# A query projection moved ahead of a wait, and key stacks sent in three lots, in a fused attention kernel

## The reference

```python
# block 0: grouped-query attention, 32 query heads, 8 key/value heads, head width 16
q = x @ Wq + bq;  k = ctx @ Wk + bk;  v = ctx @ Wv + bv
scores = einsum('bkgld,bksd->bkgls', q, k) / sqrt(16) + mask
x = layernorm(softmax(scores) @ v @ Wo + bo + x) * gamma + beta
# block 1: two cross-attentions (16 heads of width 128, one extra key and value) and a gelu MLP
x = x + cross_attention(layernorm(x), ctx)      # twice
x = x + gelu(layernorm(x) @ w_fc1 + b_fc1) @ w_fc2 + b_fc2
```

## Time and profile before

| | |
|---|---|
| median of 3 runs | 2584.45 us (2582.57 to 2584.73) |
| profiled execution | 2582.68 us |
| TensorE busy | 2501.6 us, 97% |
| VectorE busy | 1700.4 us, 66% |
| ScalarE busy | 1496.3 us, 58% |
| GpSimd busy | 1325.7 us, 51% |
| block 0's pairs, batch 0 | from about 31 to 262 us |
| block 0's pairs, batch 1 | from about 1313 to 1547 us |

### The profile page before, as it was taken

How to read it: one execution, slowest core, us unless ns; L and a number is a source line. 1 busy time by engine, 2 the same in 40 slices (tenths; PEclk the granted TensorE clock), 3 DMA queues, 4 the chain that set the end, 5 groups by cost and what they waited for, 6 DMA issues and landing times.

```text
span 2580.9 us, 53158 instructions
## 1 busy us (share of the span) xinstructions
PE 2501.6 (97%) x19500; PEld 2067.1 (80%) x19500; DVE 1700.4 (66%) x2568; ACT 1496.3 (58%) x2360; POOL 1325.7 (51%) x778
## 2 busy tenths in 40 slices
PE   7999999999999999999989999999999999999999
PEld 6666788888888888888866667888888888888877
DVE  6999676666566666665269996656665665666541
ACT  5999455555555555555459994555545555555543
POOL 1255346665644666564603553566556456655644
PEclk8999999999999999999989999999999999999999
DMA  7222134544514455452462220345444144544522
GB/s 215 72 76 78 34 100 102 130 126 103 127 46 100 100 128 130 100 128 69 144 159 68 77 70 33 100 118 130 110 119 121 36 100 113 129 116 114 128 68 66
DMA packets 86916, 263.61 MB, mean 102 GB/s; under 512 B 20544, under 2 KB 26320, under 8 KB 81120
## 3 DMA queue, kind: packets, MB, share of 16 engines
q1 hardware_dynamic: 85760, 260.80, 38.2%
q10 hardware_dynamic: 992, 0.52, 0.1%
HBM read 135.39 MB, written 8.40 MB: 56 GB/s over the span
## 4 chain that ended last, share of the span: by engine, by line
PE 80%; DVE 10%; issue 4%; ACT 2%; POOL 1%; SPq 1%; DMA 1%; DVEq 0%; POOLq 0%; ACTq 0%
PE ps_m L1110 22%; PE ps_t L1110 19%; PE ps_s L1110 16%; PE ps_m L1379 7%; PE ps_t L1379 6%; DVE sm L1719 6%; PE ps_s L1232 3%; DVE pt L1727 1%; POOL pT_lo L561 1%; PE ps_m L1312 1%; PE ps_m L1268 1%; PE ps_m L1120 1%; PE ps_t L1251 1%; SPq L474 1%; DVE nm L1719 1%
## 5 line engine op out<-in xcount | busy, mean ns | idle before, releaser
L561 POOL TENSOR_TENSOR pT_lo<-pT_lo,pT_hi 128x1024 fp32r<-128x1024 f32 x220 | 530.0, 2409 | 498.0 <-ACT pT_hi L757 486.8
L757 ACT ACTIVATE pT_hi<-pT_lo 128x1024 fp32r<-128x1024 f32 x224 | 238.0, 1062 | 326.3 <-DMA pT_lo<-pb 326.3
L901 ACT ACTIVATE p<-ps_s,nm 128x1024 f32<-128x1024 f32 x256 | 284.9, 1113 | 206.5 <-DVE nm L1789 206.1
L1786 DVE TENSOR_REDUCE nmx<-ps_s 128x1 f32<-128x1024 f32 x256 | 309.8, 1210 | 121.9 <-PE ps_s L1110 121.9
L1110 PE MATMUL ps_s<-kT,qT 128*128 128x512 f32 x1536 | 384.0, 392 | 0.3 <-ACT p L901 0.3
L1805 DVE STREAM_TRANSPOSE pb<-p 128x1024 f32<-128x1024 f32 x224 | 278.1, 1242 | 107.0 <-ACT p L901 103.1
L1110 PEld LDWEIGHTS ps_s<-kT,qT 128*128 128x128 f32 x1536 | 281.3, 188 | 55.9 <-ACT p L901 1.3
L1719 DVE CUSTOM_DVE_ANT_0 sm<-ps_s,mask 128x1024 f32<-128x1024 f32 x256 | 302.7, 1214 | 14.1 <-PE ps_s L1232 12.7
L849 ACT ACTIVATE p<-sm,nm 128x1024 f32<-128x1024 f32 x256 | 293.5, 1146 | 22.5 <-DVE nm L1719 18.1
L1110 PE MATMUL ps_t<-ctxT,wa 128*128 128x512 f32 x1080 | 256.0, 390 | 0.0
L1110 PE MATMUL ps_m<-hT,wa 128*128 128x512 f32 x1008 | 243.9, 393 | 1.1 <-ACT g L1072 0.7
(11 more groups left out here) (181 smaller groups left out, 4667.3 us busy)
## 6 DMA issues: line engine op xcount, KB each, us to landing
pT_lo<-pb SPq DMA_DIRECT2D x896, 128.0 KB, 2.3
stg_qk<-in_wqk SPq DMA_DIRECT2D x40, 1024.0 KB, 7.4
stg_vo<-in_wo SPq DMA_DIRECT2D x48, 512.0 KB, 3.6
wob<-in_wo SPq DMA_DIRECT2D x32, 512.0 KB, 3.6
stg_vo<-in_wv SPq DMA_DIRECT2D x32, 512.0 KB, 3.7
q_stack<-scr_q SPq DMA_DIRECT2D x36, 128.0 KB, 4.2
st_ctx<-in_ctxT SPq DMA_DIRECT2D x8, 512.0 KB, 6.1
mask<-in_mask SPq DMA_DIRECT2D x8, 512.0 KB, 6.2
```

Of the source, the lines that this page charges most:

```text
L561: return nc.gpsimd.tensor_tensor(out, x, f32(hi), ALU.subtract)
L757: return nc.scalar.activation(out, in_, ACT.Copy)
L901: nc.scalar.activation(p[t % 2][:], ps_s[t % 2][:], ACT.Exp, bias=nm[:, i:i + 1], scale=SCALE1, accum_out=sums[:, i:i + 1]).then_inc(exp_d ...
L1786: nc.vector.tensor_reduce(nmx[:, i:i + 1], ps_s[t % 2][:], AX.X, ALU.max, negate=True)\
```

## The change

- Query column 3 is projected right behind column 2, before TensorE waits for the first stack, and no longer between `scores0(0)` and `scores0(1)`. ScalarE's `wide(b, 5)` now stands before `exp0(0)`, and VectorE's `low_part(5)` right behind the maxima of pair 0.
- Query columns 2 and 3 swap their banks: column 2 goes to `ps_m[1]`, column 3 to `ps_m[0]`. So the second turn waits for `low_part(4)`, and the first value products, which write `ps_m[0]`, for `low_part(5)`. Both columns wait for both key tiles to be freed.
- The key slices 1, 2 and 3 are sent one at a time, each behind the query stack and mask tile of the same number: 12 transfers of a third of the size, three times.

```diff
         bank0 = [ps_m[0][:], ps_m[1][:], ps_s[0][:, 0:512], ps_s[1][:, 0:512],
-                 ps_m[0][:], ps_m[1][:]]
+                 ps_m[1][:], ps_m[0][:]]
...
-                    if i == 1:
+                    if i >= 1:
                         for k in range(2):
                             sp.wait_ge(scr_k_out[k], 16 * (b + 1))
                             apart()
-                            stack_k(sp, k, slice(1, KVP), stack_rest)
+                            stack_k(sp, k, slice(i, i + 1), stack_rest)
...
-                for i in range(3, 5):
+                for i in range(3, 6):
                     wide(b, i)
...
                 exp0(0)
-                wide(b, 5)
                 exp0(1)
...
                     if i >= 2:
-                        free(nb + i)
+                        free(nb + 3)
...
-                pe.wait_ge(w0q_lo, CT * b + 3)
-                project_q0(2)
+                for i in range(2, 4):
+                    pe.wait_ge(w0q_lo, CT * b + i + 1)
+                    project_q0(i)
...
                         elif bank_of_half[2 * t + q] == 2:
-                            pe.wait_ge(bank_free, nb + U_PROJ0 + 2)
+                            pe.wait_ge(bank_free, nb + P_Q[2] + 3)
...
-                    if e == 0 and i == 0 and u >= 1:
-                        pe.wait_ge(rb0_done, u0 + u)
+                    if e == 0 and i == 0:
+                        if u >= 1:
+                            pe.wait_ge(rb0_done, u0 + u)
+                        else:
+                            pe.wait_ge(bank_free, nb + P_Q[3] + 3)
...
                 scores0(0)
-                pe.wait_ge(w0q_lo, CT * (b + 1))
-                project_q0(3)
                 scores0(1)
...
-                        pe.wait_ge(stack_rest, 16 * 30 * (b + 1))
+                        pe.wait_ge(stack_rest, 16 * 54 * (b + 1))
...
                 for t in range(2):
                     maxima0(t)
+                low_part(5)
...
-                    if t == 1:
-                        low_part(5)
                     copied0(t - 1, 1)
```

## The result

The changed kernel took 2569.12 us (median of 5 runs, 2569.01 to 2575.00) beside 2582.57 (5 runs, 2582.09 to 2584.73) for the kernel before on the same chip: ratio 0.9949, 95% interval 0.9938 to 0.9959. That is 13.45 us or 0.5% faster; forecast were 13.6 us. Measured a second time, the same kernel gave 0.9945 (0.9932 to 0.9958). The span of the profiled execution fell from 2580.9 to 2567.3 us.

A forecast was written before the change was run, and what follows sets the result against it. VectorE was taken to set the pace, leaving only start-up losses to win: 16.6 us, less 1.0 for the instruction block and 2.0 for the clock, gives 13.6, so 2570.8 us; range 2567 to 2577.5.

The forecast's parts named there:

- The bound: First attention: VectorE sets 3.51 us a pair of score tiles; only the 6.68 and 9.47 us lost earlier can be won.
- rival D: Steady stage takes the gain back because a transfer paced otherwise ends last: 2584.4 us, chance 0.05.
- Column 3 for nothing: TensorE's 3.02 us of column 3 fit the 3.43 us stack wait; moved ScalarE and VectorE parts free; first step 3.3 us.
- The turns' wait: TensorE's 3.02 us idle before the turns of tile 1 goes, since the swapped bank needs only low_part(4).
- The block: TensorE's stop before pair 5, read as late instructions behind key transfers, shrinks to 0.5 us a batch.
- upper bound: Instruction transfer still near the end of the shorter key burst, 47.6; TensorE goes on at 50.6: a stop of 2.0 us.
- clock term: One spell of TensorE's lower clock per batch stays, 1.0 us each, 2.0 in all; bounds 0 and 4.0.
- lower bound: No stop before pair 5: the instructions are asked for earlier, with only one or two key lots ahead.
- SyncE's queue: Issuing key lots 2 and 3 adds 5.5 us each; lot 3 still lands in time for pair 16: free.
- Rival E: Lot 3 lands late and scores of pair 16 wait; slower by 0.2% if landing after 97; 2590 us, chance 0.03.
- B: Stops before pair 5 stay, not caused by key stacks; lots give nothing: 10.4 us gained, 2574 us, chance 0.27.
- C: Lots 2 and 3 delay later blocks: one new stop a batch up to 2.67 us; 6.3 gained, 2578 us, chance 0.10.

The follow-up runs named there:

- e7: Changed kernel with the banks of columns 2 and 3 not swapped, low_part(5) still early: 2570.47 us.
- e5: Changed kernel plus 20 identity transposes on TensorE between scores0(0) and scores0(1), filling its wait for pair 0's maxima: 2569.64 us.
- e1: Changed kernel with key slices sent in one burst behind query stack 1, as before, so only the projection moved: 2577.96 us, again 2583.82 us.
- e4: Changed kernel with all three key slices in one burst of 12 transfers behind query stack 2: 2570.01 us.
- e6: Changed kernel with wide(b, 5) and low_part(5) back in their old places, banks still swapped: 2570.69 us.
- e8: Changed kernel with the bank swap undone and wide(b, 5) and low_part(5) back in their old places: 2572.05 us.
- e2: Kernel before with only the key slices sent in three lots, projection not moved: 2574.14 us, again 2574.19 us.

## Why the prediction was right, point by point

**The bound.** VectorE's pace of 3.51 us and the loss before it: 16.1 us before (6.68 + 9.47), 2.86 after (1.16 + 1.70). The fall of 13.3 us is the whole gain but for 0.3 us: the span fell by 13.6. Nothing was given back later, so rival D did not come. That 13.6 were forecast and 13.45 measured is closer than the runs can be told apart: the second time it was 13.37, while its profile lost 3.31 us in place of 2.88, and the medians of the kernel before lie between 2582.18 and 2585.30. Such closeness is luck.

**Column 3 for nothing.** Right: 0.64 and 0.20 us of the wait were still left. The first step was 3.37 where 3.3 stood (in the second profile 3.36 and 3.82), and no cost of ScalarE's and VectorE's parts shows. Pair 0 of batch 0 starts at 32.68 in place of 32.32, but TensorE still waited for the stack, so column 3 isn't the cause. With it, pair 7 at 58.41 meets the forecast 58.4 partly by luck. Pair 0 of batch 1 starts 5.39 us earlier, of which 5.17 (260.18 to 255.01 for pair 63, in the same timelines) came from batch 0; 0.22 remain of the 0.49 that the faster first scores (0.73 us, as expected) were to give.

**The turns' wait.** It went, as said. The prediction put that down to the swapped banks alone; e7 shows that the early low part would have done as well.

**The block.** The range was 0 to 2.0 us a batch, 0.5 was taken, 0.23 and 0.48 were measured, and nothing above 0.16 in the second profile. The size came out, but hardly for the reason given. The upper bound had the packet at 47.6 and TensorE going on at 50.6; measured were 47.47 and 50.13, so in batch 0 the block came about when the upper bound had it. The stop was short because TensorE reached this place at 49.90 (50.13 - 0.23) and not at 48.6: pair 0 was 0.36 later, and the steps up to pair 5 had lost about 1 us before the block. The prediction's clock term stands for this loss. It and the block were added as if they came one after the other, but a TensorE that came here later waited less: 0.23 us at 17.22 behind pair 0, 1.23 at 16.19 (e5). The picture of the upper bound, a block tied to the end of the burst, nevertheless failed in e1: the packet started 9.12 us behind the burst's first issue before, and 6.81 and 5.52 there. The lower bound had a block that is asked for earlier when TensorE is earlier; no record shows the asking.

**The clock.** One spell a batch at 1.0 was the term; there was one, from 36.5 to 46 and from 1313 to 1323. What is left of the loss besides the stop is 1.16 - 0.23 = 0.9 and 1.70 - 0.48 = 1.2, and 1.40 and 1.89 in the second profile, which has no stop. So the size fits for both terms together; that all of the rest is the clock isn't shown. Its cause was named too narrowly: e5 filled the wait for the maxima, and the spell became shorter (about 6.8 us, beside 10.2 to 13.6) but stayed.

**SyncE's queue.** The term was mis-sized: 5.5 us for lots 2 and 3 became 8.20 and 7.84. It cost nothing, since pair 16 comes 11.8 us behind the last issue, and these transfers took a median of 2.8 us to land. Rival E needed a landing after 97 where this one is at about 81.

**Rivals B and C.** B's stops do depend on the key transfers: e1 has them (1.88 and 2.98 us), e4 does not. How a block is queued behind those transfers no run shows. In the steady part of the changed kernel blocks cost next to nothing (23 packets of 16 KB on queue 8 between 100 and 240 us, no "issue" gap over 0.18); in pairs 4 to 11, with the key transfers on the DMA, the stops went up to 3.51 us (e1).

C, new stops at later blocks, did not come in the two profiles of the changed kernel. But e5, e6 and e8 send the key slices exactly as it does, and have stops of 1.02, 0.49 and 1.36 us in pair 8 of one batch each. So C happens in some executions; whether it stands behind the 2571.76 and 2575.00 among the five times of the changed kernel isn't known, since these weren't profiled. The signs in the prediction are not of one mind here: by "no issue stop of over 1 us" it held, by "an issue stop stands at pairs 4 to 9" the 0.23 and 0.48 would speak against it.

**What the prediction did not see** is how the 13.6 us divide. Its rival B prices the kernel in which the move works and both stops stay at 10.4 us gained (8.4, if the spell of the clock in the first pairs is taken off as in the forecast, which the rival's sum leaves out). e1 is that kernel, and gained 4.2 and nothing: its stops were a little longer, and others came at later blocks, so its profiles lost 11.3 and 16.8 us in the two batches together, beside 16.2 before. The lots alone gave 8.0 and 9.2, where their two stops and the clock behind them stood at 6.2. On the first chip the halves add up to 12.2, on the second, where both together gave 13.4, to some 9: with the burst in place what the move gained went again in such stops (3.51 us the longest). And the clock's fall at column 3 differed between e2's two profiles, of one program. e2's head is that of the kernel before up to the first lot, and its first steps were 3.66 and 3.68 once, 5.89 and 5.80 the other time; so the 5.20 and 6.15 of the profile before were one draw of several.

## What to carry to other kernels

When an engine stops in the middle of a run of instructions that holds no wait, and the releaser is given as "issue", look for a packet of kind "instruction" on the DMA just before it goes on, and for a burst of transfers around it. Check that the engine goes on a nearly fixed time behind that packet (here 1.2 to 1.8 us), since a short wait for another engine can carry the same word. Such a burst needn't be smaller: here it was enough to send what wasn't needed yet later (e4, one stop of 0.57 us) or in pieces (e2, no stop in pair 4 to 5 above 0.21). Time an early move together with the transfers beside it: in e1 the earlier TensorE stopped for 1.88 and 2.98 us, where it had been 1.57 and 2.67. And work for which an idle stretch is free cover is better tried in front of the wait than behind it: column 3 took 2.96 or 2.97 us in front, and behind it 3.06 in e2's first profile, but 4.61 to 5.49 in the profile before and e2's second, where the granted clock had fallen to 0.50.

## What the runs showed of the hardware

A stop that I read as a wait for instructions lasted up to 3.51 us (e1). Twenty matmuls added ahead of such a stop moved it 19 matmuls earlier in the instruction stream (e5). TensorE went on 1.2 to 1.8 us after the end of a packet of 16 KB on the instruction queue, in 22 stops of 22. With nothing behind query stack 1 the packet before the stop in pair 4 to 5 started 13.8 to 14.6 us behind pair 0, with 1.15 MB there 15.6 to 16.9. Idle stretches of TensorE of the same length (3.12 and 3.09 us, e2) were followed once by granted clock 1.00 and once by 0.51 (windows from 32 to 37). Twelve transfers of 32 KB took SyncE 5.44 us to issue behind 1.3 MB of other transfers (a query stack and a mask tile) in one place and 8.20 behind the same in another. What stays open: whether and when TensorE asks for a block, how its packet is queued behind the others, why some executions have a stop in pair 8 and others not, and why the granted clock fell in e5 although the wait was filled.
